# A two-layer transformer kernel: the residual stream and the tiles counted down from it begin 64 bytes lower in SBUF

## The reference

```python
mod = (_silu(L0_c) @ L0_wmod).reshape(8, 6, 1, -1)          # per layer
h = _layernorm(x) * (1 + ca) + sa
x = x + ga * L0_attn(h, Wq, Wkr, Wdk, Wupk, Wupv, Wo)       # 32 heads of 128, 8 KV heads, causal
h = _layernorm(x) * (1 + cb) + sb
x = x + gb * L0_ffn(h, router_w, A, B)                      # 4 LoRA experts, best 2
h = _layernorm(x) * (1 + ca) + sa
x = x + ga * L1_attn(h, wq, wk, wv, wo)                     # 32 heads of 16, causal
h = _layernorm(x) * (1 + cb) + sb
x = x + gb * L1_ffn(h, base_W, base_b, router_W, router_b, A, B, expert_map)
```

## Time and profile before

| | |
|---|---|
| median of three runs | 1960.45 us |
| the profiled execution | 1953.37 us |
| its span, first to last instruction | 1951.6 us |
| mean granted TensorE clock | 0.984 |
| PE busy | 96% |
| DVE busy | 77% |
| ACT busy | 48% |
| POOL busy | 47% |
| share of L1063 in the chain that ended last | 18% |
| share of L1024 in it | 16% |

### The profile page before, as it was taken

The page is one execution under the profiler, slowest core; times in us unless marked ns, Lnnn a source line. Parts: engine busy times, 40 slices in busy tenths (PEclk is TensorE's granted clock), DMA queues, the critical chain, the costliest instruction groups (busy, mean ns, idle before and its releaser), DMA issues.

```text
span 1951.6 us, 37656 instructions
## 1 busy us (share of the span) xinstructions
PE 1875.2 (96%) x12504; PEld 1539.5 (79%) x12504; DVE 1511.6 (77%) x2386; ACT 928.2 (48%) x2297; POOL 908.6 (47%) x872
## 2 busy tenths in 40 slices
PE   8999978999999999999999999998999999998997
PEld 3688867888888888888888888886798856666776
DVE  2577747878888888888888888888789668889886
ACT  1333324444444444444444444454655378888333
POOL 0133344444444444444444444363486668887111
PEclk9999988999999999999999999998999999999999
DMA  9577741111111111111111111321387786553111
GB/s 345 177 238 246 231 153 41 49 49 49 49 49 48 48 47 41 45 43 48 48 48 48 48 48 46 95 80 62 104 239 229 232 239 181 156 158 105 43 60 60
DMA packets 201703, 211.12 MB, mean 108 GB/s; under 512 B 19066, under 2 KB 172666, under 8 KB 200604
## 3 DMA queue, kind: packets, MB, share of 16 engines
q1 hardware_dynamic: 200692, 209.27, 34.7%
q10 hardware_dynamic: 936, 0.85, 0.1%
HBM read 128.14 MB, written 73.53 MB: 103 GB/s over the span
## 4 chain that ended last, share of the span: by engine, by line
PE 71%; issue 11%; DVE 9%; POOL 4%; SPq 2%; DMA 1%; ACT 1%; POOLq 0%; DVEq 0%; ACTq 0%
PE ps L1063 18%; PE ps L1024 16%; PE ps L1037 7%; PE ps L1052 5%; PE ps L1075 4%; DVE f_neg_max L2033 4%; PE ps L1047 3%; PE ps L1849 3%; PE ps L2652 2%; POOL k_rot L571 2%; PE ps L2616 2%; PE ps L2152 2%; PE ps L2210 2%; SPq L1348 2%; PE ps L2158 1%
## 5 line engine op out<-in xcount | busy, mean ns | idle before, releaser
L1063 PE MATMUL ps<-wo,ot 128*128 (+1 forms) x1536 | 388.5, 402 | 0.0
L1063 PEld LDWEIGHTS ps<-wo,ot 128*128 128x128 f32 x1536 | 282.7, 190 | 58.7
L818 ACT ACTIVATE prob<-ps,neg_max 128x128 f32<-128x128 f32 (+1 forms) x512 | 208.6, 421 | 132.7 <-DVE neg_max L899 109.7
L1024 PE MATMUL ps<-ht_hi,wq 128*128 (+1 forms) x1024 | 255.4, 392 | 5.9 <-DVE q_swap L892 5.9
L978 POOL TENSOR_TENSOR q_rot<-q_rot,q_swap 128x512 f32<-128x512 f32 x128 | 164.8, 1288 | 180.0 <-DVE q_swap L892 175.4
L825 ACT ACTIVATE pt<-ps 128x512 fp32r<-128x512 f32 x192 | 108.1, 597 | 283.6 <-PE ps L1075 283.5
L1024 PEld LDWEIGHTS ps<-ht_hi,wq 128*128 128x128 f32 x1024 | 193.1, 189 | 48.0 <-issue 6.3
L972 POOL TENSOR_TENSOR prob<-prob,inv_sum 128x512 f32<-128x512 f32 x64 | 66.7, 1042 | 293.3 <-DVE inv_sum L908 293.3
L571 POOL TENSOR_TENSOR k_rot<-k_rot,k_swap 128x512 f32<-128x512 f32 x32 | 60.2, 1884 | 190.7 <-DVE k_swap L476 190.7
L1037 PE MATMUL ps<-pt,vv 128*128 128x512 f32 x576 | 144.5, 395 | 3.4 <-issue 2.9
L874 DVE TENSOR_TENSOR ot<-ps,ot 128x512 fp32r<-128x512 f32 x128 | 88.3, 691 | 76.4 <-ACT ot L835 76.3
(11 more groups left out here) (248 smaller groups left out, 4125.7 us busy)
## 6 DMA issues: line engine op xcount, KB each, us to landing
stack_dram<-e_part SPq DMA_DIRECT2D x192, 128.0 KB, 2.4
v_dram<-v_part SPq DMA_DIRECT2D x32, 512.0 KB, 5.9
k_dram<-k_part SPq DMA_DIRECT2D x64, 256.0 KB, 2.5
kk<-k_dram SPq DMA_DIRECT2D x128, 128.0 KB, 2.1
vv<-v_dram SPq DMA_DIRECT2D x128, 128.0 KB, 2.1
f_q<-stack_dram SPq DMA_DIRECT2D x124, 104.0 KB
f_k<-stack_dram SPq DMA_DIRECT2D x124, 104.0 KB
wmod<-in_wmod SPq DMA_DIRECT2D x12, 1024.0 KB, 12.2
```

The source lines that it names most:

```text
L818: nc.scalar.activation(p[:, h], sc[:, h], ACT.Exp, bias=neg_max[:, t, h:h + 1], accum_out=row_sum[:, t, h:h + 1]).then_inc(p_exp, 1)
L1024: mm = nc.tensor.matmul(ps_q[j][:], w[:, at:at + HD0], r[:, bass.ds(b, 2), k], start=(n == 0), stop=(n == len(passes) - 1))
L1063: mm = nc.tensor.matmul(ps_y[j][:], o[:, j, h * P:(h + 1) * P], w[:, bass.ds(at + h * D, D)], start=(n == 0), stop=(n == len(passes) - 1))
```

## The change

`keep.acc_at` is rounded so that it is 32 modulo 128: (229,344 - 32,768 - 32) // 128 * 128 + 32 = 196,512, 64 bytes below the old place. x_stream, ot0, ot1, turned1, g_raw0/g_lo0, g_raw1/g_lo1 and g_rl all begin 64 bytes lower, at 32 modulo 128. The top 64 bytes of the free space are left unused. No instruction is added, removed or moved in its order.

```diff
         keep.tokens_at = -(-nc.sbuf_base // 32) * 32
-        keep.acc_at = nc.sbuf_top - 4 * NT * D
+        keep.acc_at = (nc.sbuf_top - 4 * NT * D - 32) // 128 * 128 + 32
         keep.acc = nc.alloc_sbuf_tensor_at("x_stream", [P, NT, D], F32, offset=keep.acc_at)
```

## The result

The changed kernel takes 1948.19 us (median of six runs, 1944.83 to 1949.87) against 1957.95 for the kernel before (six runs); the ratio is 0.995, with a 95% interval of 0.9934 to 0.9967. That is 9.8 us less, between 6.5 and 12.9. Timed again later beside other kernels, the same code had a ratio of 0.9957 (0.9944 to 0.997). The forecast was 1951.7, the range 1946.3 to 1960.5.

The account below looks back on a forecast made before the run. PE's own pace was taken to bound the kernel; 7.7 + 0.3 (attention) + 0.7 (output stage) = 8.7 us off the median 1960.45 gave 1951.7 us, range 1946.3 to 1960.5.

Parts of the forecast that it names:

- What bounds the kernel: First layer's attention, 310 to 1300 us: PE busy practically every microsecond, so only its own pace sets the time.
- The chains of L1063: Attention: chains of 12 products go from 2.81 to 2.75 and 2.88 to 2.84 us; 0.13 us saved a unit, 7.7 in all.
- The output stage: L2616 and L2652 with moved tiles: 0.12 us saved an output element, 0.7 us counted, between nothing and 1.0.
- The sum: Whole kernel: 7.7 + 0.3 + 0.7 = 8.7 us saved.
- The room for a faster PE, and DVE, ACT and POOL: Attention: 0.48 us of room at L1037's second group, no other engine becomes the bound; instructions on moved tiles gain nothing.
- all of the gain between 310 and 1300 us: Sign that the prediction is right: the whole saving would appear in the first layer's attention.
- rival C: 1300 to 1388 us: longer PE pauses lower the granted clock, making the kernel slower, 1962 to 1966 us; chance 0.05.
- The reason, as I gave it: Products whose two SBUF operands lie 64 bytes apart modulo 128 are slower by 4 to 8 ns.
- Rival A: L1063: alignment is not the cause, perhaps wo's register-computed address is; no change, 1960.4 us; chance 0.22.
- Rival B: All of the excess goes, mainly in L1063: 12.7 us saved, 1947.8 us; chance 0.13.
- main forecast: Whole kernel: the likeliest case, 8.7 us saved, 1951.7 us; chance 0.60.
- Rival D: SBUF placement: the address does not move as said; excluded by arithmetic, no chance given.

Follow-up runs that it names:

- out_only: The kernel before with turned1, g_raw/g_lo and g_rl alone 64 bytes lower, x_stream and ot left in place; ratio 0.9985 (0.9974 to 0.9995).
- ot_256: The changed kernel with ot 128 bytes lower, still 32 modulo 128; profiled only, no ratio; unit of attention 16.75 us.

## Why the prediction was right

*What bounds the kernel:* right. PE was busy without a gap from 450 to 1250 us before and after, and each 0.01 us of a chain came through some 60 units to the end.

*The chains of L1063:* right in place, a little large in size. Behind L1052 the stand-in L595 said 2.75, measured 2.75. Behind the transposes L1859's said 2.84, measured 2.85 to 2.86. L1024 and L1037 behind them gave 0.02 where the prediction, from rounded differences, had 0.03. The unit lost 0.11 us and not 0.13; 59 units are 6.5 us instead of 7.7. From the first to the last L1063 it is 7.1 in the profile, against 8.0 forecast.

*The output stage:* 0.13 us an element where 0.12 was forecast. out_only as a whole measured 0.15% (0.05 to 0.26), 2.9 us, more than the 0.9 that its elements explain; its interval begins at 1.0 us, so the rest may be scatter.

*The sum:* 64 units x 0.11 = 7.0 us, as the profile has it, and 8 x 0.13 = 1.0 for the elements make 8.0, against 8.7 forecast and 9.8 timed (6.5 to 12.9; 8.6 in the second timing). What the timed medians have beyond 8.0 is less than the interval's half width, so the runs can't tell 8.0 from 8.7. The time itself, 1951.7 forecast and 1948.19 measured, was 3.5 us off, and 2.5 of this come from where the forecast started: at the median of three runs, 1960.45, where six runs have 1957.95.

*The room for a faster PE, and DVE, ACT and POOL:* right. In attention no wait took the place of the time that was gone, and ot's 691 ns stayed. The 3.6 us that the second layer's attention had more in the profile were in no term of the prediction.

*Details of the forecast that were off:* L1063's median was to be 389 to 391 ns; it is 393 in one profile of the changed kernel and 389 in the other, and 393 in ot_256, which is as slow as the kernel before. So a median was too coarse a sign, and the starts the better one. The unit was to be 16.61. And "all of the gain between 310 and 1300 us" left out the output stage, which the sum itself had at 0.7. In rival C, 85 products cost 4.9 us more than the gain, which gives 1965.3 and not 1966.

*The reason, as I gave it, was wrong in one step:* "64 bytes apart modulo 128". The rows held only pairs at the same place modulo 256, or 64 off, which can't tell 128 from 256. ot_256 does: 128 bytes apart is as slow as 64. That 196,512 fits modulo 256 was luck: the old place happened to lie 64 above one that fits. With a top of SBUF 128 bytes elsewhere, the distance would have been 192 before and 128 after. By the units of the table, 16.67 and 16.75, the same line of code would have made attention slower, by an estimated 5 us in 64 units.

*Rival A* falls: the address of wo is computed as before, and 0.11 us of the excess of a unit are gone. The Trainium skill, "SBUF — State Buffer", section "Who interferes with whom", has TensorE's two read ports independent, and by that ot's place could not matter. Here it does: the unit is 16.64 or 16.75 us with nothing else changed but where ot begins. *Rival B* (all of the excess gone, 0.19 us a unit) fell by the argument against it, getting in step: 0.11 went. That its time, 1947.8, lies nearer to the measured one than the main forecast's is chance: counted from 1957.95, the main forecast would be 1949.3 and B 1945.3. *Rival C* did not occur where it was placed: after 1300 us the granted clock was 0.96 and 0.88. A lower clock did cost the first profile some 2 us in the second layer's attention, but not the second profile of the same code. *Rival D* was excluded rightly: the tiles moved as computed. But the rounding aimed at a period of 128 that ot_256 refutes.

*Left open:* what the two reads share, or whether it is the reads at all, since only places and times were measured; why 32, 64, 128 and 224 give the same unit; why -64 costs a quarter or less in L1063 and the whole in the output stage; and whether x_stream's place has a part in the falls of the clock in the second layer's attention. Only the distance of ot and wo was scanned, and the period is shown for them alone.

## What to carry to other kernels

Where TensorE is the bound, compare the distance between the starts of equal products from line to line: 3% between two lines with the same shapes is a cause to be found. Then look at the SBUF addresses of the weight tile and of the streamed tile together, and keep their distance a multiple of 256 bytes, the one distance that was clean in every line measured here; an address in itself, or an alignment to 128, is not enough. And when a stage that a change can't reach is some us longer in one profile, compare its granted clock and take a second profile of the same code before explaining it.

## What the runs showed of the hardware that was not expected

A product of 128x128 weights and 512 columns in fp32r starts every 226.7 ns when the two tiles fit and the chain is in step, and about every 233 ns at distance 64, where the chain never gets into step. For ot and wo the dependence has a period of 256 bytes. It is not the same everywhere: in L1063 +64 costs 0.11 us a unit of 24 such products and -64 costs 0.03 (0.01 with 16 of the 24 displaced); in the output stage turning every distance of 64 round leaves the cost at 0.13 an element. Also, a misplaced chain passes its disorder on to the next line: L1037 takes 2.09 us behind ot at a distance of 128, and 2.04 at a distance of 0, with none of its own tiles moved.
